# Moving ScalarE's scale of the attention output ahead of the exponentials in the last beat of a period

## The reference

```
xn  = layernorm(x)                       # x, ctx: 16 x 128 x 1024
q   = softmax(Wq xn over the 64 of a head) * 64**-0.5     # 8 heads of 64
k   = softmax(Wk ctx over the 1024 positions)
v   = Wv ctx
out = Wo ((k v^T) q) + bo                # 128 x 1024 per batch
out = out / max(|out| over channels, 1e-12) * g * sqrt(128)
x   = x + out
x   = x + ffn(layernorm(x))              # router, top 8 of 256 slots, gate
```

## Time and profile before

| | |
|---|---|
| median of 3 runs | 719.25 us (716.36 to 720.95) |
| the profiled execution | 718.9 us, of which span 717.1 us |
| busy: PE, DVE, ACT, POOL | 647.9, 508.7, 450.4, 410.4 us |
| mean granted TensorE clock | 0.949 of full speed |
| chain that ended last | PE 87%, ACT 4%, DVE 3%, issue 3%, DMA 2% |
| DMA | 72.58 MB, mean 101 GB/s |

### The profile page before, as it was taken

The page is one execution under the profiler, slowest core; times in us unless marked ns, Lnnn a source line. Parts: engine busy times, 40 slices in busy tenths (PEclk is TensorE's granted clock), DMA queues, the critical chain, the costliest instruction groups (busy, mean ns, idle before and its releaser), DMA issues.

```text
span 717.1 us, 11885 instructions
## 1 busy us (share of the span) xinstructions
PE 647.9 (90%) x3974; PEld 563.7 (79%) x3974; DVE 508.7 (71%) x689; ACT 450.4 (63%) x896; POOL 410.4 (57%) x421
## 2 busy tenths in 40 slices
PE   5999979898998989897979797979797989999896
PEld 3788878787787878686868686868686889999574
DVE  5888967767576767685959594949594674565897
ACT  5566655756565656565656565757575676767584
POOL 4845473756565656464657575646564664452195
PEclk9999998989899999898999998989999999999999
DMA  8834452424233434232334342334232510000056
GB/s 309 187 104 111 133 154 52 135 69 118 81 104 97 109 101 107 93 104 92 107 97 110 94 112 93 105 93 106 70 77 71 141 38 1 2 1 1 1 206 264
DMA packets 52012, 72.58 MB, mean 101 GB/s; under 512 B 10112, under 2 KB 42400, under 8 KB 51696
## 3 DMA queue, kind: packets, MB, share of 16 engines
q1 hardware_dynamic: 50912, 68.07, 32.2%
q0 software_dynamic: 896, 2.45, 1.1%
q10 hardware_dynamic: 144, 1.31, 0.6%
HBM read 29.85 MB, written 8.39 MB: 53 GB/s over the span
## 4 chain that ended last, share of the span: by engine, by line
PE 87%; ACT 4%; DVE 3%; issue 3%; DMA 2%; POOL 0%; DVEq 0%; SPq 0%; ACTq 0%; POOLq 0%
PE ob L519 16%; PE gm L493 15%; PE turn L477 9%; PE q_slot L451 5%; PE q_slot L452 5%; PE q_slot L453 5%; PE gm L571 4%; PE k_slot L451 4%; PE k_slot L453 4%; PE k_slot L452 4%; PE turn L571 3%; PE gm L502 3%; DVE nkm L1162 2%; ACT o_sb L796 2%; PE turn L526 2%
## 5 line engine op out<-in xcount | busy, mean ns | idle before, releaser
L1008 POOL TENSOR_TENSOR qs_sb<-qs_sb,qrec 128x1024 f32<-128x1024 f32 x64 | 121.7, 1902 | 138.8 <-DVE qrec L1195 138.8
L519 PE MATMUL ob<-mt_sb,q_hd 128*128 128x128 f32 x1024 | 126.4, 277 | 2.6 <-issue 2.1
L519 PEld LDWEIGHTS ob<-mt_sb,q_hd 128*128 128x128 f32 x1024 | 121.8, 192 | 7.2 <-issue 5.7
L1162 DVE TENSOR_REDUCE nkm<-k_slot 128x1 f32<-128x1024 f32 x62 | 75.2, 1212 | 73.8 <-PE k_slot L453 73.8
L1181 DVE TENSOR_REDUCE qm<-q_slot 128x16 f32<-128x1024 f32 x64 | 76.0, 1188 | 68.9 <-PE q_slot L453 68.9
L755 ACT ACTIVATE ek<-k_slot,nkm 128x1024 f32<-128x1024 f32 x62 | 69.1, 1114 | 79.9 <-DVE nkm L1162 79.7
L477 PE MATMUL turn<-ident,qs_sb 128*128 128x128 f32 x512 | 75.8, 297 | 47.4 <-ACT o_sb L796 47.4
L493 PE MATMUL gm<-ekT,ctxT 128*128 128x256 f32 x512 | 118.2, 379 | 0.0
L477 PEld LDWEIGHTS turn<-ident,qs_sb 128*128 128x128 f32 x512 | 65.7, 154 | 59.2 <-ACT o_sb L796 53.1
L493 PEld LDWEIGHTS gm<-ekT,ctxT 128*128 128x128 f32 x512 | 97.1, 190 | 14.9 <-DMA ekT<-kt 0.4
L765 ACT ACTIVATE qs_sb<-qs_sb 128x1024 f32<-128x1024 f32 x64 | 68.0, 1062 | 33.1 <-DVE qs_sb L1184 33.1
(11 more groups left out here) (207 smaller groups left out, 1284.7 us busy)
## 6 DMA issues: line engine op xcount, KB each, us to landing
ekT<-kt SPq DMA_DIRECT2D x496, 64.0 KB, 2.1
ctx_in<-ctx_rows SPq DMA_DIRECT2D x16, 512.0 KB, 4.5
x_all<-x SPq DMA_DIRECT2D x16, 512.0 KB, 3.5
ctxT<-ctx_cols SPq DMA_DIRECT2D x16, 512.0 KB, 3.9
out<-q_hd SPq DMA_DIRECT2D x15, 512.0 KB, 2.6
Wuq_in<-Wuq_cols ACTq DMA_DIRECT2D x1, 1280.0 KB, 8.7
x_all<-values_cols POOLq DMA_DIRECT2D x1, 1024.0 KB, 8.4
ekT<-kt POOLq DMA_DIRECT2D x16, 64.0 KB, 4.4
```

Of the source, the lines that this page charges most:

```text
L519: last = nc.tensor.matmul(ob[:, (j % 4) * C:(j % 4 + 1) * C], q, mt_sb[:, b % 2, t, :], start=(t == 0), stop=(t == T - 1))
L1008: nc.gpsimd.tensor_tensor(e, e, qrec[:, i % 2, :].unsqueeze(2).broadcast_to([P, PAIR, DH]), ALU.mult).then_inc(q_mul, 1)
L1162: V.tensor_reduce(nkm[:, i:i + 1], k_psum(b, i)[:, :], AX, ALU.max, negate=True).then_inc(k_max, 1)
```

## The change

In ScalarE's program the call of `o_scale` goes from the third place of beat 3 to the first, ahead of `q_exponential(p, 2)`, `k_exponential(b, 3)` and `q_copy(p, 1)`. Nothing else changes: no instruction is added or taken away, and all waits stay with their instructions. `q_exponential` and `k_exponential` of that beat now stand behind `o_scale`'s wait for `o_turn`.

```diff
             for b in range(PERIODS):
                 p, o, e = b - 1, b - 2, b - 3
                 for i in range(4):
+                    if i == 3 and 0 <= e < RESIDUAL_BY_VECTOR:
+                        o_scale(e)
                     if i == 0 and has(o):
                         mt_scale(o)
...
                     if i == 1 and 0 < b and has(b + 1):
                         ctx_high(b + 1)
-                    if i == 3 and 0 <= e < RESIDUAL_BY_VECTOR:
-                        o_scale(e)
                     qb, qi = (p, i - 2) if i >= 2 else (o, i + 2)
```

## The result

The changed kernel takes 640.78 us in the median of four runs (640.1 to 641.72), against 719.2 us; the ratio is 0.891 (95% interval 0.888 to 0.895). The profiled execution took 641.72 us, of which 639.9 us are the span (before: 718.9 and 717.1). Its mean granted clock is 0.997.

What follows compares the result with a forecast made beforehand. TensorE's turn of q waited for a slot held until ScalarE's late scale, which also lowered the clock. 718.9 - 78.2 (47.4 idle, 30.8 clock) + 1.2 (stall in period 16) = 641.9 us; range 636 to 658.

Steps and rivals of the forecast that it cites:

- The slot was the wait: Turn of q in beat 3: 13 waits for ScalarE's scale, 47.4 us idle, vanish; beats take 6.63 us.
- The clock: 13 last beats: clock returns to 1.00 once TensorE's idle time goes; gain between nothing and 30.8 us, upper taken.
- The term of 30.8 us: 13 last beats: matrix work at the lower clock, the part of the 78.2 us gain beyond 47.4 us idle.
- The delay of q's exponential: ScalarE, beat 3: q's exponential comes 1.10 us later, covered by 1.7 us of VectorE's maximum; price nothing.
- GpSimd: Scale of q's last quarter: begins near 5.1 us, ends near 7.0 in the period; margin 1.6 us, price nothing.
- The one stall in period 16: Second turn of q, without a k tile as cover, waits for GpSimd's scale: about 1.2 us (0 to 2).
- The k moves: Second half of a k move: turn of k must come 4.4 us later to be felt; price nothing.
- The cap from busy time: Whole kernel: TensorE busy 647.9 of 717.1 us would limit the time to 649.7 us; the prediction rejected it.
- the blocked ScalarE: Rival, head of beat 3: scale waits for the output's turn and delays the exponentials; 733.2 us, chance 0.03.
- the new wait: Rival, each period: GpSimd's scale of the last quarter comes late, 1 to 2 us; 655 to 668 us, chance 0.11.
- the clock came back in full: Answers the rival that the beats still run at the lower clock without idle time: 672.7 us, chance 0.03.
- the wait was the slot's: Answers the rival that q's turn waits for something else ending with the scale: 719 us, chance 0.03.

Runs made afterwards that it cites:

- the second set: The changed kernel itself run again beside the kernel with the quarter first in period 16, nothing changed: median 643.72 us.
- three different places of the scale: Against the kernel before, scale moved to the head of beat 3 (640.78 us), behind q's exponential (640.81 us) or the end of beat 2 (640.93 us).
- the filled kernel: Order of the kernel before, with 31 unused transposes of the identity on TensorE in the wait: 691.34 us, ratio 0.965.
- the kernels with copies: Scale behind q's exponential as in the second place, with two or three unused ScalarE copies ahead of it: 666.04 us and 686.74 us.
- the second place: Against the kernel before, scale moved behind q's exponential and ahead of k's exponential in beat 3: 640.81 us, ratio 0.896.

## Why the prediction was right

The forecast was 641.9 us on the profiled execution; it took 641.72. The mechanism and the terms are borne out one by one below; that the two numbers meet within 0.2 us is luck in part. The four executions of that set lie between 640.1 and 641.72 us and those of the second set between 640.38 and 646.65, and in the profiled one the beats gave 0.5 us less than forecast while the stretch ahead of period 3, which the change does not touch, was 0.9 us shorter.

- **The slot was the wait, and nothing else stood behind it.** Shown: with the slot free in time the wait is gone, in three different places of the scale, and each of 13 beats is 6.66 us, where the beat of period 2 had given 6.63. The 0.03 us make 0.4 us of the sum.
- **The clock.** That it would come back with the idle time is shown by the filled kernel. The term of 30.8 us was mis-sized. It put down to the clock all that the wait did not explain. A beat with the old wait and the full clock is 6.66 + 3.65 + 0.22 = 10.53 us by the kernels with copies, and 10.51 us in the filled one, so the clock's share is 164.38 - 13 x 10.53 = 27.5 us, and 13 x 0.22 = 2.9 us are the lost overlap and the slower turn after a wait. These 27.5 us are a remainder; the filled kernel gives the clock's share by itself, 164.38 - 13 x 10.51 = 27.8 us. The sum was not hurt, since the three go together: 47.4 + 2.9 + 27.5 = 77.8 us.
- **The delay of q's exponential costs nothing.** Shown by the second place and by the cover of 1.6 us in the timeline.
- **GpSimd.** Walked: the last quarter from 5.1 to 7.0 us into the period; measured 4.93 to 6.83. The margin of 1.6 us is 1.8.
- **The one stall in period 16** was put at 1.2 us and is 0.94.
- **The k moves** were given a margin of 4.4 us in a common period, and there is no wait for them in any. In period 16 there is none left, which the prediction did not walk; it is hidden under the 0.94 us.
- **The cap from busy time**, 649.7 us, was passed by 8 us in the profiled execution (641.72 us). TensorE's busy time fell from 647.9 to 616.4 us with the same 3974 matmuls:

```profile
PE 616.4 (96%) x3974; PEld 541.8 (85%) x3974; DVE 507.4 (79%) x689; ACT 446.1 (70%) x896; POOL 409.3 (64%) x421
```

Of the rivals, the blocked ScalarE was brought about, and the cover held; the new wait appeared nowhere but in period 16; the clock came back in full; and the wait was the slot's, as its length followed the scale's place in five kernels.

## What to carry to other kernels

When one engine waits for another, look at whether the late instruction had its input long before: if so, its place in its own engine's order is the fault, and the nearest place ahead of the instruction that waits will do if the result is then in time. Here the second place was enough: the scale ended 0.36 us before the turn began. Price such a wait by a stretch of the same trace where the wait doesn't occur, not by its length alone, and not by busy time: here 47.4 us of waiting were worth 77.7 us. Before moving an instruction up, name the reader of each one that it delays, and how long that reader is busy with other things.

## What was not expected

Filling a wait with useless matrix work made the kernel before 25.6 us faster (0.965 of its time), by holding the granted clock at 1.00.

The clock's answer to a wait differs from one to the next though the waits are alike, and it does so in a regular order: of 13 waits of 2.72 us every third, four in all, was followed by a fall, and waits of 3.65 us were followed by beats at 0.74 in seven periods and at 0.86 in six, about 1.2 us apart.

Executions of the same kernel differ by more than its loop does: the changed kernel had a median of 640.78 us in one set and of 643.72 us in the other, where two executions took about 641 us and two about 646. In the profiled execution of the second set (645.83 us) the 13 beats are 6.66 us again; of the 4.1 us by which its span is longer, 2.8 are lost before period 3, where the clock was 0.83 between 20 and 40 us and 1.00 in the first set's profile.
